# Storing the gated feed-forward values of a token side by side

## What is computed

```python
def bit_linear(x, w):                      # values: one scale per token, weights: one scale
    return einsum('bsd,hd->bsh', act_quant(x), weight_quant(w))
def act_quant(x):
    scale = 127.0 / clip(max(abs(x), axis=-1), 1e-05)
    return clip(round(x * scale), -128, 127) / scale
...
h = bit_linear(x, w1)                      # 256 -> 1024 hidden features
h = depthwise_conv1d(h, conv_w, conv_b)    # three taps along the tokens
h = silu(h)
return bit_linear(h, w2)                   # 1024 -> 256
```

## Time and profile before

| | before |
|---|---|
| median of three runs | 844.23 us (842.24 to 848.17) |
| profiled execution | 845.46 us, its span 843.6 us |
| TensorE busy | 773.1 us (92%) |
| VectorE busy | 596.0 us (71%) |
| ScalarE busy | 440.7 us (52%) |
| GpSimd busy | 379.4 us (45%) |
| granted TensorE clock, mean | 0.952 |

### The profile page before, as it was taken

The page is one execution under the profiler, slowest core; times in us unless marked ns, Lnnn a source line. Parts: engine busy times, 40 slices in busy tenths (PEclk is TensorE's granted clock), DMA queues, the critical chain, the costliest instruction groups (busy, mean ns, idle before and its releaser), DMA issues.

```text
span 843.6 us, 21269 instructions
## 1 busy us (share of the span) xinstructions
PE 773.1 (92%) x7399; PEld 715.3 (85%) x7399; DVE 596.0 (71%) x1446; ACT 440.7 (52%) x1047; POOL 379.4 (45%) x515
## 2 busy tenths in 40 slices
PE   4999999999999975699998999999999999999674
PEld 4999999999999965699997988988888888888464
DVE  0467776777777763144331468899999999999994
ACT  1444455444445432122221657777777777776552
POOL 1434545545555442222214766466666666653100
PEclk8999999999999986699998999899999999999788
DMA  5325321100000214577730000000000000000000
GB/s 174 99 65 205 61 58 17 25 9 9 8 9 15 64 41 35 160 219 216 208 104 21 10 13 10 8 16 15 16 16 15 15 15 16 14 9 8 10 12 14
DMA packets 27442, 43.30 MB, mean 51 GB/s; under 512 B 10549, under 2 KB 21722, under 8 KB 26826
## 3 DMA queue, kind: packets, MB, share of 16 engines
q1 hardware_dynamic: 17930, 33.03, 14.6%
q0 software_dynamic: 5808, 5.63, 3.0%
q10 hardware_dynamic: 3600, 3.28, 1.1%
HBM read 34.04 MB, written 7.88 MB: 50 GB/s over the span
## 4 chain that ended last, share of the span: by engine, by line
PE 56%; DVE 25%; issue 11%; DMA 4%; ACT 2%; POOL 1%; SPq 1%; DVEq 0%; ACTq 0%; POOLq 0%
PE bank_h L1533 5%; PE bank_b L1495 4%; PE bank_e L1507 4%; PE bank_d L1533 4%; PE bank_f L1507 4%; PE bank_g L1518 4%; PE bank_e L1691 3%; PE bank_c L1544 3%; PE bank_f L1691 3%; PE bank_c L1703 3%; PE bank_c L1484 2%; PE bank_d L1703 2%; DVE diff L926 2%; PE bank_a L1484 2%; DVE w L1241 2%
## 5 line engine op out<-in xcount | busy, mean ns | idle before, releaser
L484 POOL TENSOR_TENSOR qbd<-qt,consts_f 128x560 f32<-128x560 f32 x128 | 163.0, 1279 | 184.5 <-PE bank_e L1507 95.8
L633 ACT ACTIVATE pt<-bank_g 69x448 f32<-69x448 f32 x128 | 69.4, 542 | 34.7 <-PE bank_h L1518 33.3
L627 ACT ACTIVATE prob<-diff 112x345 f32<-112x345 f32 x128 | 62.0, 485 | 39.1 <-DVE diff L926 39.1
L1533 PE MATMUL bank_h<-values,pt 69*69 69x68 f32 x1024 | 76.4, 229 | 2.5 <-ACT pt L642 2.5
L1533 PEld LDWEIGHTS bank_h<-values,pt 69*69 69x69 f32 x1024 | 71.8, 146 | 3.0 <-ACT pt L633 3.0
L1533 PEld LDWEIGHTS bank_d<-values,pt 69*69 69x69 f32 x1024 | 70.5, 142 | 2.2
L1507 PEld LDWEIGHTS bank_e<-kt,qbd 128*112 128x112 f32 x640 | 71.0, 178 | 1.4
L1533 PE MATMUL bank_d<-values,pt 69*69 69x68 f32 x1024 | 71.8, 226 | 0.0
L1518 PE MATMUL bank_g<-consts_f,prob 112*69 112x112 f32 x512 | 71.5, 262 | 0.0
L1507 PEld LDWEIGHTS bank_f<-kt,qbd 128*112 128x112 f32 x640 | 71.1, 178 | 0.0
L1507 PE MATMUL bank_e<-kt,qbd 128*112 128x69 f32 x640 | 70.9, 258 | 0.0
(11 more groups left out here) (205 smaller groups left out, 1938.7 us busy)
## 6 DMA issues: line engine op xcount, KB each, us to landing
w<-in_w SPq DMA_DIRECT2D x25, 512.0 KB, 4.1
w<-in_w SPq DMA_DIRECT2D x1, 4096.0 KB, 15.0
patches<-in_patches SPq DMA_DIRECT2D x16, 222.0 KB, 2.6
expert_results<-prob ACTq DMA_DIRECT2D x25, 128.0 KB
expert_rows<-x SPq DMA_DIRECT2D x16, 138.0 KB
out<-h SPq DMA_DIRECT2D x16, 138.0 KB
f_raw<-in_f SPq DMA_DIRECT2D x2, 1024.0 KB, 7.8
wqkv<-in_wqkv SPq DMA_DIRECT2D x2, 768.0 KB
```

Source lines behind the costliest of these rows:

```text
L484: pool.tensor_tensor(qbd[u % 2][:], q.broadcast_to([128, NG, HPB, QG]), head_mask.unsqueeze(1).unsqueeze(3).broadcast_to([128, NG, HPB, QG ...
L627: act.activation(prob[u % 2][:], diff[u % 2][:], ACT.Exp, scale=DH ** -0.5).then_inc(S["prob_made"], 1)
L633: act.activation(pt[u % 2][:, :, 0:4, :].rearrange("t h g q -> t g h q"), banks["g"][0:T, 0:4 * SR].rearrange("t (g h q) -> t g h q", g=4, ...
L1533: ins = mm(heads_out[b][:, hd * (DH + 1):(hd + 1 + AHEAD) * (DH + 1)], pt[u % 2][:, i, :, :].rearrange("k g q -> k (g q)")[:, 0:T], values ...
```

## The change

`z` becomes a densely packed view [128, sequence b, token t, chunk j]: the eight chunks of a token are adjacent. The tangent goes into a buffer `th` of its own, with the old order; the two tap buffers move up one place. The gate reads `th` and `yc` in the old order and writes `z` in the new one, so that neighbouring elements that it writes lie 32 bytes apart. `hidden_max`, `scale_gated` and `round_up` go through `z` as it lies. `round_down` reads `z` as it lies and writes `zb` in its old order, so that neighbouring elements that it writes lie 280 bytes apart. `tanh` no longer waits for the roundings of the pair before (`z_int`) but for its gate (`z_made`); the gate waits for `z_int` of the pair before.

```diff
--- before.py
+++ after.py
@@ -267,8 +267,9 @@
         ffn = w1[:].rearrange("p e c n -> p (e c n)")
         NW = HFC * 2 * TP
         cut = lambda i: ffn[:, i * NW:(i + 1) * NW].rearrange("p (j b t) -> p j b t", j=HFC, b=2)
-        hs, yc, z = cut(0), cut(1), cut(2)
-        taps = [cut(4), cut(5)]
+        hs, yc, th = cut(0), cut(1), cut(4)
+        z = ffn[:, 2 * NW:2 * NW + 2 * T * HFC].rearrange("p (b t j) -> p b t j", b=2, t=T)
+        taps = [cut(5), cut(6)]
         zb = ffn[:, 3 * NW:3 * NW + NW // 2].bitcast(BF16).rearrange("p (j b t) -> p j b t", j=HFC, b=2)
         f_raw = [sb("f_raw1", [128, KC * HF]), sb("f_raw2", [128, HFC * D])]
         f_abs = sb("f_abs", [128, 2])
@@ -803,14 +804,14 @@
             def round_up(p):
 
                 act.wait_ge(BK["d"], read_after(order, "d", "spread2", p))
-                act.activation(z[:, :, :, 0:T], z[:, :, :, 0:T], ACT.Identity,
+                act.activation(z, z, ACT.Identity,
                                bias=cf[:, CF.at("rounding")][:, 0:1]).then_inc(F["z_rounded"], 1)
 
             def round_down(p):
 
                 act.wait_ge(F["z_rounded"], p + 1)
                 wait(act, F["ffn_made"], p)
-                act.activation(zb[:, :, :, 0:T], z[:, :, :, 0:T], ACT.Identity,
+                act.activation(zb[:, :, :, 0:T].rearrange("p j b t -> p b t j"), z, ACT.Identity,
                                bias=cf[:, CF.at("rounding")][:, 1:2]).then_inc(F["z_int"], 1)
 
             def scale_results(p):
@@ -825,8 +826,8 @@
             def tanh(p):
 
                 act.wait_ge(F["conv_added"], 2 * (p + 1))
-                wait(act, F["z_int"], p)
-                act.activation(z[:, :, :, 0:T], yc[:, :, :, 0:T], ACT.Tanh, scale=0.5).then_inc(F["tanh_made"], 1)
+                wait(act, F["z_made"], p)
+                act.activation(th[:, :, :, 0:T], yc[:, :, :, 0:T], ACT.Tanh, scale=0.5).then_inc(F["tanh_made"], 1)
 
             def move_quantized(p):
 
@@ -1225,21 +1226,20 @@
             def gate_hidden(p):
 
                 dve.wait_ge(F["tanh_made"], p + 1)
-                rows = lambda v: v[:, :, :, 0:T].rearrange("p j b t -> p (j b) t")
-                dve.scalar_tensor_tensor(rows(z), rows(z), 1.0, rows(yc), ALU.add, ALU.mult).then_inc(F["z_made"], 1)
+                wait(dve, F["z_int"], p)
+                dve.scalar_tensor_tensor(z.rearrange("p b t j -> p j b t"), th[:, :, :, 0:T], 1.0, yc[:, :, :, 0:T], ALU.add, ALU.mult).then_inc(F["z_made"], 1)
 
             def hidden_max(p):
 
                 dve.wait_ge(F["z_made"], p + 1)
                 wait(dve, F["max_turned"], p)
-                dve.tensor_reduce(zmax[:], z[:, :, :, 0:T].rearrange("p j b t -> p b t j"), X, ALU.max,
+                dve.tensor_reduce(zmax[:], z, X, ALU.max,
                                   apply_absolute_value=True).then_inc(F["zmax_made"], 1)
 
             def scale_gated(p):
 
                 dve.wait_ge(F["spread2_made"], p + 1)
-                dve.tensor_tensor(z[:, :, :, 0:T], z[:, :, :, 0:T],
-                                  spread_cols[1].rearrange("p (b t) -> p b t", b=2).unsqueeze(1).broadcast_to([128, HFC, 2, T]),
+                dve.tensor_tensor(z, z, spread_cols[1].rearrange("p (b t) -> p b t", b=2).unsqueeze(3).broadcast_to([128, 2, T, HFC]),
                                   ALU.mult).then_inc(BK["d"], 1)
 
             def add_projected(p):
```

## The result

The changed kernel takes 907.21 us (four runs, 906.69 to 910.39) against 844.74 us for the kernel before in the same series. The ratio is 1.0744, with a 95% interval of 1.0714 to 1.0775. The forecast was 845 us, the range ended at 862. The profiled execution took 910.39 us, its span 908.6.

What follows compares the result with a forecast made beforehand. VectorE was taken to bound the kernel, TensorE 0.7 us behind. Terms of -1.1, +0.7, +0.5 and -0.1 summed to 0.0 us, meaning the 844.23 us median again; the forecast said 845 us, range 834.5 to 862.

Steps and rivals of the forecast that it cites:

- What bounds the kernel: Layer 1 pass of 21.1 us: VectorE, busy 21.07 us, sets the pace, with TensorE only 0.7 us behind.
- Part 1: VectorE's reduction, now over adjacent elements, should take 1264 ns against 2058, 0.79 us less for each of 16 pairs.
- Part 2: VectorE's gate, writing 32 bytes apart, should lose 0.71 us, taking 2.0 us instead of 1.30; size not shown.
- the read price: Extra per element for scattered VectorE reads, 0.64 or 0.72 ns; the gate's writes were priced at 0.64 once.
- Rival 1: A scattered write costs twice a scattered read: gate +1.42 us, 855 to 856 us in all; chance 0.35.
- Part 3: VectorE's `scale_gated`, now adjacent and reading each scale eight times over, should cost nothing extra; upper bound 0.10 us.
- Part 4: ScalarE's `round_down`, writing bfloat16 280 bytes apart, should take 0.75 us more, 1.98 us instead of 1.23.
- the cover: Extra `round_down` time on ScalarE that should not delay VectorE's gate: 0.78 us a pass, 0.22 near the end.
- Part 5: The new waits of the gate (for `z_int`) and of `tanh` (for an earlier gate) should cost nothing.
- The sum: Passes 6 to 19 -1.1, pass 5 +0.7, thin cover in pass 19 +0.5, passes 20 and 21 -0.1: 0.0 us.
- The range: Whole kernel time from 834.5 to 862 us; within it 0.48, faster 0.15, slower 0.37.
- Rival 2: Scattered writes are free: VectorE saves 0.79 us a pass, -10.4 us in all, 834 us; chance 0.18.

Runs made afterwards that it cites:

- Experiment 8: Changed kernel with only chunks j and j + 4 adjacent, in gated and rounded values alike, gate writing 8 bytes apart: 834.78 us, ratio 0.9889.
- experiment 3: Kernel before plus 22 ScalarE and 16 VectorE dense or scattered instructions on spare buffers behind the last product; only durations count: scattered 4-byte write and read 2.15 us on ScalarE.
- experiment 7: Changed kernel with rounded values in adjacent chunk pairs, so the second rounding writes runs of two bfloat16 elements 552 bytes apart: 849.02 us, ratio 1.0056.
- experiment 2: Changed kernel with the second rounding reading 32 bytes apart and writing adjacent bfloat16 values: 855.08 us, ratio 1.0143.
- Experiment 4: Kernel before with only the second rounding changed, reading 560 bytes apart and writing bfloat16 280 bytes apart: 908.64 us, ratio 1.0768.
- experiment 1: Changed kernel with rounded bfloat16 values written densely in the new order, TensorE reading weights 16 bytes apart: 848.68 us, ratio 1.0054.
- experiment 5: Kernel before, old layout, reduction replaced by three maxima of adjacent elements, two moved to the end of the pass before, magnitudes left out: 849.4 us, ratio 1.0072.

## Why the prediction was wrong, point by point

- **What bounds the kernel:** right. VectorE sets the pass and TensorE is 0.7 us behind. Experiment 8 took 0.77 us from VectorE and got 0.53 of it.
- **Part 1, the reduction:** right, -0.77 us (0.79 forecast).
- **Part 2, the gate:** right in kind and near in size: +0.87 us (0.71 forecast), by experiment 3 the read price once. Rival 1's double price isn't there. The Trainium skill, page "Vector Engine (DVE) Microarchitecture Reference", section "Measured stream behaviour on trn2", has 2.50 ns a column for a writing step of 24 words. No run here has that step; at 8 words the gate pays 0.79 ns on top of about 1.03 (estimated from 682 ns for 512 elements, L1250, and 1292 for 1104, L1242), so 1.8 ns.
- **Part 3, `scale_gated`:** right, 1292 ns.
- **Part 4, ScalarE, is the step that failed.** Its mechanism held: what the rounding exceeds the cover by stalls VectorE one to one (gate waits of 0 in experiment 7, 0.16 in experiment 2 and 2.92 us in the change, for 0.04, 1.11 and 3.92 us more rounding). The cover is 0.95 to 1.0 us, not 0.78. What failed is the term for the rounding: +0.75 us with an upper bound of 1.59, measured +3.92. The bound came from scattered reads of 4 bytes and was carried over to writes of 2 bytes as if only the number of hops counted. The width of what each hop writes counts more: 3.5 ns an element at 2 bytes against 0.8 at 4. Experiment 4 shows that this term alone makes the result.
- **Part 5, the waits:** right; no wait for `z_int` shows.
- **The sum** has a second, smaller miss. It let gate and reduction cancel to -0.08 us a pass, wherever they stand in it. Without the dear write the pass is 0.25 us longer than before (experiment 7), and the kernels of experiments 1 and 7 are 4.6 and 6.0 us above before instead of level. The gate's loss stands in front of what TensorE waits for, the reduction's gain behind it.
- **The range:** its upper end took in the double price for VectorE and half of it for ScalarE. It had no term for TensorE's clock either. The clock fell in the change and in experiment 4 (mean 0.92) and not in experiment 1 (0.957), so it follows the long rounding; that TensorE's idle time is the link is likely and not shown. The three passes at the lowest clock took 1.1 to 1.5 us more than the others, and the last product 1.7 us more.
- **Rival 2:** wrong for this layout. Its 834 us is near what experiment 8 measured, but that is luck: the write is free there because its neighbours lie 8 bytes apart, and rival 2 held every scattered write to be free.

## What to carry to other kernels

When a layout moves, price each operand by its neighbours in the order in which the instruction walks, and by the width of the element, on every engine that touches the buffer, the narrowing conversion included. Before choosing between two full transpositions look for a layout in between: here pairs brought every read and write of the VectorE and ScalarE operations back to the dense price, with the same number of instructions. Look also at where in the pass a gain and a loss stand: they cancel only if no other engine waits for something between them. A bound for an operand that the trace doesn't show must come from a row that has the same width and the same side, or be much wider.

## What the runs showed of the hardware

All for 1104 elements over 128 partitions, ScalarE / VectorE, dense 1.21 / 1.31 us:

| access | 4 B | 8 B | 16 B | 32 B | 280 B and more |
|---|---|---|---|---|---|
| float32, one word at a time, written | dense | 1.28 / 1.31 | 2.23 / 2.11 | 2.27 / 2.15 | 2.15 / 2.03 |
| float32, one word at a time, read | dense | 1.28 / 1.31 | 2.24 / 2.10 | 2.27 / 2.14 | 2.15 / 2.04 |
| bfloat16, one element at a time, written | 1.52 / 1.38 | 2.74 / 2.61 | 5.17 / 5.05 | 4.93 / 4.79 | 5.04 / 4.93 |
| runs of two, bfloat16 or float32, written | | | | | 1.23 to 1.24 / 1.31 |

- A lone 2-byte write 16 bytes or more from the last costs 3.2 to 3.6 ns extra, some four times what a lone 4-byte one costs (0.65 to 0.96), on both engines. Runs of two adjacent ones, 552 bytes apart, cost next to nothing extra.
- TensorE loads bfloat16 weights at 4 bytes apart in 113 ns, as dense, and at 16 bytes apart in 223 ns, most of it behind the products.
- A VectorE operation of two elements took 1.10 us instead of 0.14 beside a GpSimd operation (experiment 5), and a GpSimd operation of 1.14 us took 1.86 and 2.61 us when it started inside a VectorE operation of 1.29 and 2.17 us. The cause was not isolated.
